# A mixture-of-experts stage on one core: first tile of each expert at a fixed place, its up products in three passes

## The reference, cut to what matters

```python
scores = softmax(t @ gate_w.T)                 # 896 x 16
weights, indices = top_k(scores, 2)
for e in range(16):                            # INTER = 352
    w_e = sum(where(indices == e, weights, 0))
    y = y + (silu(t @ w1[e].T) * (t @ w3[e].T)) @ w2[e].T * w_e[:, None]
z = (silu(t @ sw1.T) * (t @ sw3.T)) @ sw2.T    # shared, 704 wide
out = x + tanh(g_ffn[1]) * (y + z)
```

## Time and profile before

| | |
|---|---|
| time, median of 3 runs | 949.61 us (947.12 to 950.68) |
| the profiled execution | 949.65 us, its span 948.0 us |
| busy: TensorE, VectorE, ScalarE, GpSimd | 919.7, 471.5, 319.1, 80.2 us |
| DMA, whole span | 96.05 MB, of it 22.35 MB on GpSimd's queue |
| one tile's DMA | load 1408 + 512 + 192 KB, gather 257 KB, store 256 KB |
| last scatter issued / first gather issued | 737.22 / 743.11 us |
| first rows copied to xg / transposed by TensorE | 749.28 / 753.77 us |
| span ends | 948.0 us, last tile's copy to yr at 930.96 us |

### The profile page before, as it was taken

One profiled execution on the slowest core, in us unless ns is written; L12 is line 12 of the kernel. 1 busy time (PEld: TensorE's weight loads), 2 busy tenths in 40 slices (PEclk: granted clock), 3 DMA queues, 4 the chain that ended last, 5 costly groups with the idle time before them and its releaser, 6 DMA issues.

```text
span 948.0 us, 18170 instructions
## 1 busy us (share of the span) xinstructions
PE 919.7 (97%) x7600; PEld 733.1 (77%) x7601; DVE 471.5 (50%) x778; ACT 319.1 (34%) x494; POOL 80.2 (8%) x110
## 2 busy tenths in 40 slices
PE   5999999999999999989999999999999999999996
PEld 5878787878787878779999888887798765665654
DVE  6665545454554546784344344798656122222225
ACT  4633332333323333664433210444542221222210
POOL 0000000000000002210000000013005111222211
PEclk9999999999999999999999999999999999999999
DMA  9001010001020103049700100700502449977716
GB/s 338 19 24 34 1 35 1 35 1 34 2 78 2 34 2 112 1 126 281 250 0 1 45 1 1 272 2 1 183 1 112 170 136 334 332 237 254 259 63 236
DMA packets 26774, 96.05 MB, mean 101 GB/s; under 512 B 3282, under 2 KB 4306, under 8 KB 23634
## 3 DMA queue, kind: packets, MB, share of 16 engines
q1 hardware_dynamic: 19490, 71.11, 21.7%
q0 software_dynamic: 6352, 22.35, 7.1%
q10 hardware_dynamic: 864, 1.57, 0.4%
HBM read 76.37 MB, written 18.66 MB: 100 GB/s over the span
## 4 chain that ended last, share of the span: by engine, by line
PE 85%; DVE 7%; ACT 3%; DMA 2%; issue 2%; POOL 0%; SPq 0%; DVEq 0%; POOLq 0%; ACTq 0%
PE ps L570 18%; PE ps L571 16%; PE ps L572 16%; PE ps L1002 10%; PE ps L1012 5%; PE ps L650 4%; PE ps L633 4%; PE ps L836 2%; PE ps L837 2%; PE ps L838 2%; PE ps L993 1%; DVE arena L1709 1%; PE ps L672 1%; DMA land_c<-in_ctx 1%; DMA token_rows<-arena,to_row 1%
## 5 line engine op out<-in xcount | busy, mean ns | idle before, releaser
L570 PE MATMUL ps<-arena_r 128*125 128x512 f32 (+1 forms) x416 | 163.7, 393 | 3.6 <-DVE arena_r L1390 3.6
L571 PE MATMUL ps<-arena_r 128*125 128x512 f32 (+1 forms) x416 | 156.8, 377 | 0.0
L572 PE MATMUL ps<-arena_r 128*125 128x512 f32 (+1 forms) x416 | 156.6, 377 | 0.0
L570 PE MATMUL ps<-hT,arena_r 128*128 128x448 f32 (+1 forms) x368 | 136.7, 372 | 2.4 <-DVE arena_r L1409 1.1
L572 PE MATMUL ps<-hT,arena_r 128*128 128x448 f32 (+1 forms) x368 | 134.9, 367 | 0.0
L571 PE MATMUL ps<-hT,arena_r 128*128 128x448 f32 (+1 forms) x368 | 134.8, 366 | 0.0
L1002 PE MATMUL ps<-arena 128*128 x336 | 102.9, 459 | 0.0
L1073 ACT ACTIVATE arena<-arena,mbias,mscale 125x448 f32<-125x448 f32 x96 | 66.2, 752 | 101.9 <-DVE arena L1517 101.9
L570 PEld LDWEIGHTS ps<-arena_r 128*125 128x125 f32 (+1 forms) x416 | 77.9, 187 | 21.2 <-DVE arena_r L1390 4.0
L572 PEld LDWEIGHTS ps<-arena_r 128*125 128x125 f32 (+1 forms) x416 | 77.7, 187 | 13.8
L1002 PEld LDWEIGHTS ps<-arena 128*128 128x128 f32 x336 | 62.3, 190 | 31.2
(11 more groups left out here) (237 smaller groups left out, 1259.7 us busy)
## 6 DMA issues: line engine op xcount, KB each, us to landing
arena<-in_e SPq DMA_DIRECT2D x16, 1408.0 KB, 7.0
arena<-in_e SPq DMA_DIRECT2D x16, 512.0 KB, 8.2
sorted_rows<-arena POOLq DMA_DIRECT2D x1, 7453.0 KB, 57.3
land_c<-in_ctx SPq DMA_DIRECT2D x8, 752.0 KB, 4.3
arena<-sorted_rows POOLq DMA_DIRECT2D x21, 257.0 KB, 6.5
land_w<-in_gu SPq DMA_DIRECT2D x8, 512.0 KB, 17.1
arena<-in_e SPq DMA_DIRECT2D x16, 192.0 KB, 9.3
land_d<-in_wd SPq DMA_DIRECT2D x1, 2816.0 KB, 34.3
```

The costliest lines, as they stand in the source:

```text
L570: mm(into, a[0], w[0], start=i == 0, stop=False)
L571: mm(into, a[0], w[1], start=False, stop=False)
L572: last = mm(into, a[1], w[0], start=False, stop=i == len(operands) - 1)
```

## The change

- Every expert gets tile e as its first tile, at a fixed place (tile number = expert number); what exceeds 128 rows goes to overflow tiles 16, 17, ... behind. `expert_end` is gone; at least two overflow tiles are run. This run has 21 tiles either way.
- Slots go by tile number. SP loads one set of weights per tile; for overflow tiles in a loop, which reads the expert from `tile_expert` and waits for each load to land before the next turn.
- The up products of tiles 0 to 15 go in three passes of split operands (`up_first`). For that ScalarE copies high halves of the weights (`expert_high`, 2 parts of 1408 columns) and of the rows (`rows_high`), VectorE makes the low halves (`expert_low`, `rows_low`). Overflow tiles keep whole float32.
- The three loops start with tile 16 (ScalarE's with 15); the tiles before are written out, with a new order on VectorE and ScalarE.
- First and second place of a pair now go by the row's place, and the first-half rows are gathered back when all tiles but the last are stored.

```diff
@@ block.sync
-            for e in range(2, NE):
-                if e - 2 + NSLOT < NE:
-                    last = sp.value_load(expert_end[0:1, e - 2:e - 1], min_val=1, max_val=ROWS_MAX)
-                    post(e)
-                    sp.wait_ge(d_mm, last)
-                    load_expert(e - 2 + NSLOT)
...
+            for e in range(NSLOT, NE):
+                sp.wait_ge(d_mm, e - 3)
+                load_expert(e)
+                post(e - 1)
+            post(NE - 1)
...
+            with sp.Fori(NE, tiles) as n:
+                e = sp.value_load(tile_expert[0:1, bass.ds(n, 1)], min_val=0, max_val=NE - 1)
+                w = A_E + n % NSLOT * 4352
+                sp.wait_ge(d_mm, n - 3)
+                sp.dma_start(arena[:, bass.ds(w, 2816)], e13_in[bass.ds(e, 1)].rearrange("o p w -> p (o w)")
+                             ).then_inc(e_ld[0], 16)
...
+                sp.wait_ge(e_ld[0], 48 * (NE // NSLOT) - 48 * (NE - 1) + n * 48)
+                sp.sem_inc(w_landed, 1)
-            for j, landed in enumerate((last, tiles)):
+            for j, landed in enumerate((last1, tiles)):
@@ block.tensor
+            def up_first(e):
+
+                pe.wait_ge(w_low, nth("sh2") + 2 * e + 2)
+                pe.wait_ge(ln_T, 4 * NT + e + 1)
+                for j in range(2):
+                    last = product(ps[:, 4 + j, 0:EI], [([half[:, k, :] for half in xgT_r], piece(e13[e], k, j * EI, EI))
+                                                        for k in range(KC)])
+                last.then_inc(gu_mm, 1)
...
-            with pe.Fori(1, last1) as n:
+            for n in range(1, NE):
+                up_first(n)
+                rows_T(n + 1)
+                down_expert(n - 1)
+                hidden_T(n)
+            with pe.Fori(NE, last1) as n:
@@ block.scalar
+            def expert_high(e):
+
+                act.wait_ge(w_landed, e + 1)
+                if e >= 2:
+                    act.wait_ge(gu_mm, e - 1)
+                elif e == 1:
+                    act.wait_ge(scattered, 16 * 2 * NT)
+                for part in e13_part[e]:
+                    fn(part[0], part[2], ACT.Copy).then_inc(w_high, 1)
...
+            for n in range(NE - 1):
+                expert_high(n + 1)
+                silu_tile(n)
+                rows_high(n + 1)
+                place(n + 2)
+            with act.Fori(NE - 1, last2) as n:
@@ block.vector
+            def expert_low(e):
+
+                for i, part in enumerate(e13_part[e]):
+                    dve.wait_ge(w_high, nth("sh2") + 2 * e + i + 1)
+                    v.tensor_tensor(part[1], part[2], part[0].bitcast(F32), ALU.subtract).then_inc(w_low, 1)
...
+            for n in range(NE):
+                if n >= 1:
+                    tile_hidden_save(n - 1)
+                if n + 1 < NE:
+                    expert_low(n + 1)
+                tile_hidden(n)
+                if n + 1 < NE:
+                    rows_low(n + 1)
+                row_ends(n + 1)
+                if n == 0:
+                    shared_out(BEFORE - 1)
+                else:
+                    tile_out(n - 1, n * 16 - 16 if n >= 2 else None)
```

More of the change, by code:

```diff
@@ L51 @@
 ROWS_MAX = 29
+EXTRA_MIN = 2
 ROW = D + 2
@@ L228, in flamingo @@
         land_s = landing("land_s", A_SH, 2 * KC * SHARED)
-        sh13 = [halves(23808 + m % SPARE * 1024, A_SH + 2 * KC * SH_AT[m], land_s, 2 * KC, SH_CHUNKS[m])
+        sh13 = [halves(19456 + (m + 2) % SPARE * 1024, A_SH + 2 * KC * SH_AT[m], land_s, 2 * KC, SH_CHUNKS[m])
                 for m in range(6)]
-        sh2 = halves(19440, 37120, landing("land_2", 37120, 6 * D), 6, D)
-        A_HL = [A_SH + m * 1024 for m in range(4)] + [22512, A_HT]
+        sh2 = halves(23792, 37120, landing("land_2", 37120, 6 * D), 6, D)
+        A_HL = [A_SH + m * 1024 for m in range(4)] + [26864, A_HT]
         land_h = [land_s] * 4 + [landing(f"land_h{m}", A_HL[m], TOK) for m in (4, 5)]
@@ L239, in flamingo @@
         A_E = A_KV - 16
+        A_W = [A_E + i * 4352 for i in range(NSLOT)]
+        land_e = [landing(f"land_e{i}", A_W[i], 2816) for i in range(NSLOT)]
+        e13 = [halves((4352, 28144)[e % 2], A_W[e % NSLOT], land_e[e % NSLOT], KC, 2 * EI) for e in range(NE)]
+        e13_part = [[tuple(half[:, 2 * i:2 * i + 2] for half in e13[e]) for i in range(2)] for e in range(NE)]
         h3_row = at(28144, NT, ROW)
@@ L1787, in _ @@
             dve.wait_ge(ids_set, 1)
[L1788 to L1791, removed]
             experts = iota16.unsqueeze(1).broadcast_to([P, NT, NE])
@@ L1822, in _ @@
                 dve.wait_ge(dest_set, j + 1)
-            then(v.tensor_copy(expert_end[:], ends))
+            for j in range(2):
+                then(v.tensor_tensor(ends_of[:, j, :, 0], fdest[j], fdest[1 - j], ALU.is_gt))
+                v.scalar_tensor_tensor(ends_of[:, j, :, 0], ends_of[:, j, :, 0], float(TOK), ids[:], ALU.mult, ALU.add
+                                       ).then_inc(ends_set, 1)
             for i in range(4):
-                then(v.tensor_scalar(tile_count[:, i:i + 1], ends[:, NE - 1:NE], float(i - 3), None, ALU.add))
@@ L1826, in _ @@
-            c4 = cmp.rearrange("p (n e) -> p n e", n=32)
-            then(v.tensor_tensor(c4, iota29.unsqueeze(2).broadcast_to([P, 32, NE]),
-                                 ends.unsqueeze(1).broadcast_to([P, 32, NE]), ALU.is_ge))
+                then(v.tensor_scalar(tile_count[:, i:i + 1], ends[:, NE - 1:NE], float(EXTRA_MIN), float(NE + i - 3),
+                                     ALU.max, ALU.add))
+            c4 = cmp[:, 0:NE * NE].rearrange("p (n e) -> p n e", n=NE)
+            then(v.tensor_tensor(c4, iota_x.unsqueeze(2).broadcast_to([P, NE, NE]),
+                                 ends.unsqueeze(1).broadcast_to([P, NE, NE]), ALU.is_ge))
@@ L1847, in shared_out @@
                                        ).then_inc(y_sv, 1)
-            for t in range(BEFORE - 1):
+            def expert_low(e):
+                for i, part in enumerate(e13_part[e]):
+                    dve.wait_ge(w_high, nth("sh2") + 2 * e + i + 1)
+                    v.tensor_tensor(part[1], part[2], part[0].bitcast(F32), ALU.subtract).then_inc(w_low, 1)
+            shared_out(0)
+            expert_low(0)
+            for t in range(1, BEFORE - 1):
                 shared_out(t)
```

97 lines of the change are left out of this document (50 added, 47 removed).

## The result

The changed kernel takes 960.92 us (median of 4 runs, 955.88 to 964.89) where the kernel before, run beside it, takes 948.93: a ratio of 1.0127, 95% interval 1.009 to 1.0163, so 12.0 us slower.

A forecast was written before the change was run, and what follows sets the result against it. TensorE was taken to bound the kernel before, with the DMA engines near. Changes of -2.1 us up to tile 4, +6.2 in tiles 4 to 15, +0.9 in the overflow and +1.3 in the tail sum to +6.3: 956.0 us, range 943 to 964.

The forecast's parts named there:

- the middle: Tiles 4 to 15: twelve tiles at 8.6 us against TensorE's 8.08 before, adding 6.2 us.
- the overflow: Overflow tiles: five more loads, one after another at 10.1 us; tile 20 at 922.5 against TensorE's own 921.6, +0.9 us.
- rival A: The forecast's own case, chance 0.50: store and gather loops set 8.3 to 8.9 us a tile; 953 to 959 us.
- Price of a pass, and the vector work: First tiles: 0.162 us per pass, 7.24 us a tile on TensorE; weight splitting 2.7 us on ScalarE, 3.3 on VectorE.
- The start: Up to tile 1: tile 0 starts as before, tile 1 at 763.5 us, against 763.93 before.
- the added routing steps: VectorE steps for row places ahead of the scatter: hidden, costing nothing, or 2 us if that cover were gone.
- the gathers back beside the last store: Tail: first-half row gathers wait until all but the last tile is stored: +1.3 us, bounds 0 and about 5.
- I take 8.6: Period of tiles 4 to 15, put at 8.6 us, next to the store loop's measured mean of 8.67.
- The lower bound of the same step: Least period of tiles 4 to 15: 7.65 us of work for all 16 DMA engines per tile.
- Rival C: Chance 0.25: the DMA engines are the bound, tiles reach 7.7 us; 948.7 us, or 944.2 with quicker single-file loads.
- Rival D: Chance 0.17: the late store holds the operand splitting on VectorE; 9.1 us a tile gives 961.0 us, up to 965.
- Rival B: Chance 0.08: TensorE stays the bound, first tiles at 7.24 us and overflow tiles at 8.08; 937.8 us.

The follow-up runs named there:

- run 7: run 4 without loading the down weights of experts 4 to 15 (704 of 2112 KB each), so part of the computation changes; 938.22 us, ratio 0.9892.
- run 9: run 3 (whole float32 up products) without loading the down weights of experts 4 to 15, so part of the computation changes; 950.66 us, ratio 1.0019.
- run 1: The changed kernel with overflow loads written out, a semaphore per slot, and SP's count reads moved behind them; 951.35 us, ratio 1.0027.
- run 5: run 4 with two row buffers used in turn and the loops of VectorE and GpSimd written out; 947.26 us, ratio 0.9986.
- run 3: The changed kernel with whole float32 up products in every tile and the overflow loads written out; 950.71 us, ratio 1.0029.
- run 4: run 1 with ScalarE starting once an expert's up weights have landed; only the down products wait for the rest; 950.12 us, ratio 1.0017.
- run 2: The changed kernel with whole float32 up products in every tile and no operand splitting, overflow loads still in single file; 960.28 us, ratio 1.0119.
- run 11: run 4 with down weights laid out by partition, loaded in one transfer of 128 rows of 6 KB; 950.95 us, ratio 1.0028.
- run 10: run 5 with down weights laid out by partition, loaded in one transfer of 128 rows of 6 KB; 948.76 us, ratio 1.0001.
- run 6: run 5 without loading the down weights of experts 4 to 15, so part of the computation changes; 938.3 us, ratio 0.9893.

## Why the prediction was right, and where its steps were not

The forecast was 956.0 us with 943 to 964 around it, slower as the likeliest sign; 960.92 came. That the total lies in the range is in part luck: two of its terms, the middle (-4.8 us) and the overflow (+10.9), were wrong in opposite directions, and the 953 to 959 of the forecast's own rival A misses the time. In the profiled run:

| step | forecast, us | measured, us | error |
|---|---|---|---|
| tile 1 starts | 763.5 | 766.41 | +2.9 |
| tile 1 to tile 4 | 22.6 | 22.66 | 0 |
| tiles 4 to 16 | 12 x 8.6 = 103.2 | 98.4 (8.20 each) | -4.8 |
| tile 16 to tile 20 | 33.2 | 44.1 | +10.9 |
| tile 20 to the end | 30.5 + 1.3 = 31.8 | 31.6 | -0.2 |
| span | 954.3 | 963.2 | +8.9 |

*Price of a pass, and the vector work: right.* 0.162 was forecast and 0.16 seen, 7.24 and 7.20 to 7.25 a tile; ScalarE 2.64 for 2.7, VectorE 3.16 for 3.3 (the earlier trace rows carried this). By this term alone TensorE gains 0.84 x 16 = 13.4 us, and runs 7 and 9 show that this gain is real where the loads are a third smaller: 12.0 us.

*The start: not settled.* The first gather is issued at 745.11 in the kernel after, at 743.75 in run 1 and at 741.87 in run 5, three kernels that do the same ahead of it, and at 743.11 before. So a good part of the +2.9, and of the 4.0 by which this execution lies above its median, may be the spread of executions. That the added routing steps are hidden fits (741.87 is earlier than before) but was not tried by itself. Runs 3 and 9, bound by TensorE in every tile, are still 0.29% and 0.19% above the kernel before, 1.8 to 2.8 us. In their profiles 1.4 and 1.2 of it come after the start of tile 20 (the gathers back beside the last store, forecast 1.3); the rest I can't place.

*Tiles 4 to 16: the mechanism half named, the size too large.* The step that failed is "I take 8.6". It took the pace of the store's loop from four steps of the earlier trace rows, and four are few: over fifteen steps of run 3 the same loop beside the same loads has 8.16, and in run 4, with the short tiles of three passes, 8.19. So the loop is real and is what ends last in run 4, but its pace is 8.2, and it goes with how full the DMA engines are: a store takes 5.8 to 7.3 us in run 4 and 5.6 in run 7. The lower bound of the same step is confirmed: 7.65 us of DMA work per tile from the earlier trace rows, and 0.93 x 74 us over nine tiles after the change is again 7.65. That alone puts 7.24 out of reach. Why it is 8.2 (8.0 in run 4, 7.9 in run 5) and not 7.65 is in part open. At a mean share of 0.93 to 0.96 some transfer came late every few tiles, and the order on ScalarE and VectorE passed it on to TensorE; gating ahead of the next expert's halves, or a fifth slot for weights, was not tried. Rival C (the DMA engines are the bound) named the right resource and took it to be fillable to 1.00; 7.65 at the share of 0.93 that was measured makes 8.2. The forecast also looked at the store and the gather and took the landing of the weights only for the way into the pace, tile 4; yet of the late transfers it is the one that fills the chain after the change. Runs 1, 4 and 5 show the others taking its place. Only the last step between them, 2.9 us, is clear of the noise.

*Overflow: right place, far too small.* Single file was in the sum, at 10.1 us a load from the earlier trace rows, and it was set against TensorE's own 32.3 us so that 0.9 was left of it. Up to the landing of the load of tile 19 (forecast 872.0 + 4 x 10.1 = 912.4, measured 920.3) the 7.9 us are: load 15 landed 2.1 late; 4.0 us in which SP read its counts and the next expert, which was in no term, though the change puts these reads ahead of the loop; and four turns of 10.6 in place of 10.1. The last us is TensorE's clock (below). Run 1 prices the single file and the reads together at 9.6 us, run 3 against run 2 at 9.6 as well. The place was right, but a term that is the difference of two nearly equal chains (922.5 against 921.6) has the error of both; the forecast gave it no range of its own.

*Rival D (0.17, 961 to 965)* gives the measured time by another way, a late store that holds the split for 9.1 us a tile. That is not what happened: the tiles took 8.2, and that its number fits is chance. *Rival B* was excluded rightly, and run 7 shows the one condition under which it holds, a third fewer bytes.

The Trainium skill (DMA: Bandwidth & Descriptors, section on where 436 GB/s comes from) has some 358 GB/s as what a core's HBM side gives. The rows of the experiments with the DMA engines 93 to 96% busy show 329 to 345 GB/s over ten tiles, reads and writes together. But short stretches go well above it, 392 GB/s from 820 to 826 us and 445 from 924 to 926, so the forecast was wrong to read the 364 of the earlier trace rows as agreement with a limit near there:

```profile
924.00:926.00 2.00, 2.00 (x5) 1.11 (x4) 0.00 (x0) 0.00 (x0) 0.00 (x0) 0.50 1.04 445
```

Its section on queues, rings and completion order would have the store of small rows wait for the load's large packets; run 11 was to show it. What the profile counts as packets are nearly all rows here, and the load's are twice as large in the mean as in run 4 (7.7 and 4.1 KB), but the largest, the 11 KB rows of the up weights, are the same in both. The store lands in 6.5 us there and in 6.6 in run 4, and the times (950.95 and 950.12 us) differ by no more than the noise. So no run here shows that the size of the rows ahead matters, and the test is a weak one.

## What to carry to other kernels

Before an engine's work is cut, work out how much of every shared resource one period holds: here 7.65 us of DMA work in a tile of 8.08 left TensorE at most 0.43 us to gain, and in the kernel after it gained none of it. In these runs the mean share of the DMA engines over ten tiles stopped at 0.93 to 0.96 (over 2 us it reads up to 1.11, so it is no exact gauge), and each wait that was removed was followed by the next transfer on the same engines. A wait for each load's landing in a loop costs the transfer's latency per turn, not its bandwidth (10.6 against 7.6 to 8.1 us); several semaphores, one for each slot, give it back. Of the runs that do the whole computation only 5 and 10 are level with the kernel before, and none is measurably faster; what paid with three passes is fewer bytes per tile, in runs 6 and 7, which leave down weights out. A way to it that keeps the computation, such as one load for an expert's two tiles as in the kernel before, was not tried.

## What the runs showed of the hardware that was not expected

```profile
920.00:922.00 2.00, 1.53 (x3) 1.04 (x4) 0.00 (x0) 0.00 (x0) 0.33 (x1) 0.50 0.34 131
922.00:926.00 4.00, 4.00 (x9) 2.25 (x8) 0.00 (x0) 0.00 (x0) 0.18 (x1) 0.50 0.80 290
926.00:928.00 2.00, 2.00 (x8) 1.26 (x7) 0.00 (x0) 0.00 (x0) 0.00 (x0) 0.90 0.93 364
```

A wait of 3.8 us so costs 6.8. After 0.56 us (908.34) it was 5.00, nearly nothing. In the middle the clock fell once in the kernel after, following the wait of 1.34 us at 829.55, and once in run 1, following 1.73 us; after waits of up to 1.65 us in runs 4, 5, 10 and 11 it stayed at 1.00. The clock is part of why TensorE's busy time did not fall: 919.7 us again, with 13.4 us less work in it. The slow records add up to some 6.5 us; the rest of the 13.4 was not looked into. Run 1, without the waits in the overflow, has 911.6, and run 7, with hardly a wait, 904.9.

**A store of 256 KB by rows** takes 3.0 us alone, 5.6 in the median beside loads at a DMA share of 0.79 (run 7), 5.8 to 7.3 at 0.94 (run 4). **Four values read by SP** from a table took 2.8 us, 874.11 to 876.9.
